# Attention in slots: the transposes of the probabilities one slot later and behind the pieces

## The reference

```python
qkv = x @ w_qkv                       # 32 query heads, 8 key and value heads, 16 features each
xq, xk = rope(xq), rope(xk)
scores = einsum('bhsd,bhtd->bhst', xq, repeat(xk, 4)) / sqrt(16)
scores = where(causal, scores, -inf)
probs = softmax(scores)
out = einsum('bhst,bhtd->bhsd', probs, repeat(xv, 4))
y = out @ w_o
...
x = x + layernorm(y)
x = x + layernorm(linear(layernorm(x)))
```

## Time and profile before

| | us |
|---|---|
| median of 3 runs | 1770.59 (1770.57 to 1771.24) |
| the profiled execution | 1775.06 |
| its span, first to last instruction | 1773.3 |
| TensorE busy in the span | 1657.3 (93%) |
| VectorE | 1081.9 (61%) |
| ScalarE | 796.5 (45%) |
| GpSimd | 607.9 (34%) |

### The profile page before, as it was taken

The page is one execution under the profiler, slowest core; times in us unless marked ns, Lnnn a source line. Parts: engine busy times, 40 slices in busy tenths (PEclk is TensorE's granted clock), DMA queues, the critical chain, the costliest instruction groups (busy, mean ns, idle before and its releaser), DMA issues. The chain is left out here.

```text
span 1773.3 us, 26150 instructions
## 1 busy us (share of the span) xinstructions
PE 1657.3 (93%) x8965; PEld 1384.0 (78%) x8965; DVE 1081.9 (61%) x2298; ACT 796.5 (45%) x1723; POOL 607.9 (34%) x792
## 2 busy tenths in 40 slices
PE   5999999999999999999999999988999999999884
PEld 4898987888888888777877887867877878778773
DVE  7888876525566554674243324557776877777772
ACT  4676764222233222222122222137777777776860
POOL 5465553211111112341111112374354344444422
PEclk9999999999999999999999999989999999999996
DMA  3100001000111101321011012200000000000000
GB/s 123 34 25 13 14 30 46 25 24 22 30 35 33 35 23 46 110 75 51 22 31 40 28 36 65 60 24 13 1 13 1 13 7 7 13 1 13 13 7 19
DMA packets 32967, 54.26 MB, mean 31 GB/s; under 512 B 3840, under 2 KB 9120, under 8 KB 32832
## 3 DMA queue, kind: packets, MB, share of 16 engines
q1 hardware_dynamic: 32832, 52.55, 9.8%
HBM read 43.10 MB, written 9.44 MB: 30 GB/s over the span
## 5 line engine op out<-in xcount | busy, mean ns | idle before, releaser
L1266 POOL TENSOR_TENSOR m_a_lo<-m_prod,m_a_hi 128x512 fp32r<-128x512 f32 x100 | 134.5, 1345 | 638.4 <-ACT m_a_hi L1348 638.4
L1342 ACT ACTIVATE m_prod<-a_ps 128x512 f32<-128x512 f32 x100 | 59.9, 599 | 544.9 <-PE a_ps L128 544.8
L1501 DVE TENSOR_TENSOR m_prod<-m_prod,a_ps 128x512 f32<-128x512 f32 x100 | 68.8, 688 | 386.1 <-ACT m_prod L1342 386.1
L2058 ACT ACTIVATE t_p<-a_ps,t_nmax 128x128 f32<-128x128 f32 (+1 forms) x512 | 181.8, 429 | 96.5 <-DVE t_nmax L2155 96.3
L2155 DVE TENSOR_REDUCE t_nmax<-a_ps 128x2 f32<-128x512 f32 (+1 forms) x192 | 131.6, 685 | 50.2 <-PE a_ps L2238 27.6
L2161 DVE TENSOR_TENSOR t_pT_lo<-a_ps,t_pT_hi 128x512 fp32r<-128x512 f32 x192 | 131.3, 684 | 44.5 <-ACT t_pT_hi L2051 44.1
L2244 PE MATMUL a_ps<-consts,t_p 128*128 128x128 f32 x768 | 119.9, 279 | 23.1 <-ACT t_p L2058 21.7
L2244 PEld LDWEIGHTS a_ps<-consts,t_p 128*128 128x128 f32 x768 | 87.4, 141 | 47.2 <-ACT t_p L2058 41.5
L128 PE MATMUL a_ps<-m_hT_hi,m_w_lo 128*128 128x512 f32 x312 | 124.0, 397 | 0.0
L126 PE MATMUL a_ps<-m_hT_hi,m_w_hi 128*128 128x512 f32 x312 | 123.1, 395 | 0.4 <-DVE f_w_lo L1406 0.4
L127 PE MATMUL a_ps<-m_hT_lo,m_w_hi 128*128 128x512 f32 x312 | 123.3, 395 | 0.0
(11 more groups left out here) (287 smaller groups left out, 4688.8 us busy)
## 6 DMA issues: line engine op xcount, KB each, us to landing
m_raw<-in_w_mlp SPq DMA_DIRECT2D x75, 256.0 KB, 2.7
a_xt<-in_x SPq DMA_DIRECT2D x8, 512.0 KB, 3.8
t_yl<-in_x SPq DMA_DIRECT2D x16, 256.0 KB, 4.5
x_store<-stream SPq DMA_DIRECT2D x4, 1024.0 KB, 5.2
t_yl<-x_store SPq DMA_DIRECT2D x16, 256.0 KB, 2.7
out<-t_yl SPq DMA_DIRECT2D x16, 256.0 KB, 2.0
m_raw<-in_w_attn SPq DMA_DIRECT2D x10, 256.0 KB, 2.8
a_att<-in_w_mixer SPq DMA_DIRECT2D x8, 256.0 KB, 2.8
```

What stands on the lines that cost most here:

```text
L1266: pool.tensor_tensor(a_lo[:, n % 2, :], prod[:, :], f(a_hi[:, n % 2, :]), ALU.subtract).then_inc(lo, 1)
L1501: dve.tensor_tensor(prod[:, :], prod[:, :], ps[:, U + TURN_AT["unit", n, 0] % 2, :], ALU.mult).then_inc(prodd, 1)
L2058: last = act.activation(p[:, u % 2, h * width:(h + 1) * width], unit_bank(u)[:, h * width:(h + 1) * width], ACT.Exp, bias=nmax[:, u % 3, h ...
```

## The change

TensorE's loop issues the transposes of unit s-1 at the end of slot s, behind the slot's pieces, where it issued those of unit s ahead of the pieces. In the list for the first batch, the transposed stack q(2, 0, 0) stands in slot 3 and not in slot 4. Nothing else changes; the programs of the other engines are as they were, apart from what follows from that list.

```diff
-         0: (("q", 1, 0, 0),), 1: (("q", 1, 1, 0),), 4: (("q", 2, 0, 0),), 6: (("q", 2, 1, 0),)}
+         0: (("q", 1, 0, 0),), 1: (("q", 1, 1, 0),), 3: (("q", 2, 0, 0),), 6: (("q", 2, 1, 0),)}
...
                 scores(s + 1)
             if 0 <= s - PT_RING < SLOTS:
                 values(s - PT_RING)
-            if 0 <= s < SLOTS:
-                transposes(s)
             for what, part, t, b in JOBS[s]:
                 job = name_of(what, part, t, b)
...
                 else:
                     project(what, part, t, b, bank_of(job))
+            if 0 <= s - 1 < SLOTS:
+                transposes(s - 1)
```

## The result

The changed kernel takes 1988.97 us (median of 4 runs, 1986.01 to 2002.34) against 1770.91: ratio 1.124, 95% interval 1.122 to 1.126. The profiled execution took 1988.51, its span 1986.7. The forecast was 1940, with a range that ended at 1985: the direction and most of the size are right, and the time lies 4 us above the range.

The account below looks back on a forecast made before the run. TensorE was taken to bound, with VectorE and ScalarE near three quarters busy. Six middle batches +150, the first +9 and the last +10 make 169 us: 1944 profiled, 1940 for the median, range 1890 to 1985.

Parts of the forecast that it names:

- What bounds, and the order of the chain: Attention stage: TensorE bounds, busy 65.1 of 70 us; pieces would wait for slot-end transposes, `high`, exponentials and the predecessor's copy.
- The cost of one chain: From a slot's scores issue to its piece: ready 2.13 to 3.34 us later by reader, against 0.90 or 1.02 without waiting.
- The unhindered slots: Slots 0, 7, 8, 13 and 23 of a middle batch: the predecessor piece is older, so added wait 0.
- The clock: Attention stage: TensorE keeps the full clock, as scores, values and projections run between all new waits.
- the forecast's 95.0: Length of a middle batch in us: 61.6 of TensorE's own work plus 33.4 of waits, 25.1 more than before.
- Rival 1: Slots 14 to 18, without projections, fall to half clock: 24 us, doubled if neighbours fall too, 1964 to 1988; chance 0.12.
- The suspicion named beside it: TensorE's clock: a cited skill page says transposes don't count as busy work as matmuls do; no row tells them apart.
- The ends: First batch +9; last batch +10, made of 9 for its slots and about 1 for a delayed ending.
- The moved stack: q(2,0,0) of the first batch, slot 4 to 3: the 1.45 us wait goes, included in the first batch's +9.
- The range: Whole kernel: 1890 to 1985 us, from 17 waits each 0.3 shorter or longer (1905, 1975), widened by a piece of rivals.

## Why the prediction was right and where it failed

Slots are measured here on TensorE, from the start of one mask matmul to the next one's, as medians of the six middle batches. The forecast's figure for a slot is the sum of its terms for TensorE's work and its waits in that slot.

- **What bounds, and the order of the chain**: right. ScalarE's wait for the transposes went from 0.9 to 351 us, TensorE's for exponentials from 21.7 to none, and moving the readers a slot later took the whole loss away.
- **The cost of one chain**: right to 0.1 us in slots at full clock. Measured against the sum of the forecast's terms: slot 3 4.78 and 4.76, slot 4 3.09 and 3.09, slot 5 4.66 and 4.59, slot 9 5.23 and 5.11, slot 15 3.87 and 3.79, slot 22 4.66 and 4.71. That the exponentials are a link of it was shown by moving them out: of the slots behind ScalarE, 15, 17 and 21 lost 0.7 to 1.0, what they were priced at, and those behind VectorE nothing.
- **The unhindered slots** 0, 7, 8, 13 and 23: 8, 13 and 23 are unchanged. Slot 7 took 3.1 instead of 2.67, as the half clock of slot 6 reaches into it. Slot 0 took 2.0 instead of 1.7 at full clock, so a wait of 0.2 to 0.5 stands there that the forecast had at nothing.
- **The clock**: this is the step that failed. The forecast kept the full clock "since scores, values and projections run in between all the new waits". The clock record has 35 stretches at half clock in the six batches, six a batch and five in one: they begin in slots 1, 6, 10, 12, 16 and 18, behind waits of about 2 us (that of slot 16 behind the wait in slot 15), and make up a fifth of the time. Half clock then doubles the awaited piece and the transposes behind it, on the path. Those slots are also where the forecast is short: slots 6 and 7 by 1.7 us together, 10 by 1.2, 12 by 1.6, 16 by 0.9, 18 by 1.1, 1 by 0.4. That is 6.9 of the 7.2 us by which a batch exceeds the forecast's 95.0. Of these 7.2, 5.0 went on average when the waits were filled with work, and 6.1 in the two batches where the clock never fell.
- **Rival 1** named the mechanism at 0.12 and put it into the slots without projections, at 24 us. It was right for two of its five slots, 16 and 18. It was wrong for the others: 14, 15 and 17 kept the full clock, while 6, 10 and 12, which have projections, were hit hardest. The loss of some 40 us in the six batches lies near its upper price (twice 24, 1988), which it gave for the neighbours falling too; the time of 1989 meets that figure partly by luck, as the places differ. The suspicion named beside it, that transposes don't hold the clock, is not borne out: filling the pauses with transposes kept it, so it was the pauses that cost it.
- **The ends**: the first batch's +9 was 11, the last one's +9 was 12, and the ending's +1 was 5. In the ending TensorE stood at half clock for 31 us instead of 28; how much of the 4 us this makes is not shown. The stage's start, 9 us earlier in the profiled execution, hides as much of the misses: by luck the span exceeds its forecast by 44 us, not by 53.
- **The moved stack**: right, 1.4 us in slots 3 and 4 of the first batch.
- **The range**: it allowed 0.3 us a wait, where most slots at full clock were off by 0.1 or less (slots 0 and 18 by 0.2), and took in only a part of the clock's rival, which came in at its full price.

With the clock full all through a batch (the third and the sixth of the run with added matmuls) 1.1 us are left above the forecast, spread over many slots: 0.2 in slots 0 and 18, about 0.1 in 1, 6, 9, 16 and 19, less elsewhere. Open stays where the clock falls: in the changed kernel slots 5, 9, 15, 17, 21 and 22 have waits of 1.5 to 2.2 us too, and no half-clock stretch of a middle batch begins in them. No run changes one wait at a time.

## What to carry to other kernels

When an instruction of one engine is moved, look at the fixed programs of the engines that read it: the price is what stands **behind** the reader in its queue, and whether the mover itself waits for any of that. A whole loop may be moved by a slot for nothing if its readers are moved with it; moved alone, it closed a ring. And once a change brings pauses of 2 us onto TensorE in slot after slot, price the half clock behind them too: here that was about 1.1 us each time (6.9 us for the six falls of a batch).

## What was not expected of the hardware

- Work added to TensorE made the changed kernel faster: four redundant matmuls of 0.23 us in each of 12 slots, hidden in waits, brought the granted clock from 0.90 to 0.98 and the time from 1989 to 1964 us.
- TensorE's clock fell again and again although the engine was busy for 72% of the stage and never waited for more than 2.2 us at a time in the six middle batches. Ahead of the fall in the ending of the kernel before it was busy for 47%.
- 128 by 128 float32 transposes kept the clock up like matmuls: 0.98 with either.
